# Two-layer gated cross-attention with routed experts: the last, partial chunk of keys packed by head, and its one odd key weighed by VectorE

## The reference, cut to what matters

```python
# M = 1601 context rows of 192, H = 16 heads of DH = 16
q = (x @ Wq + bq).reshape(B, N, 16, 16)
k = (y @ Wk + bk).reshape(B, M, 16, 16)
v = (y @ Wv + bv).reshape(B, M, 16, 16)
attn = softmax(einsum('bnhd,bmhd->bhnm', q, k) * 0.25, axis=-1)
out = einsum('bhnm,bmhd->bnhd', attn, v).reshape(B, N, 256)
```

## Time and profile before

| what | value |
|---|---|
| median of 3 runs | 1448.31 us |
| profiled execution, its own time | 1448.28 us |
| its span in the trace | 1446.5 us |
| PE, ACT, DVE busy (share of the span) | 92%, 68%, 41% |
| mean granted TensorE clock | 0.963 |
| attention of layer 0, first exp to last | 66.5 to 464.7 us |
| attention of layer 1, first exp to last | 765.7 to 1186.5 us |

### The profile page before, as it was taken

The page is one execution under the profiler, slowest core; times in us unless marked ns, Lnnn a source line. Parts: engine busy times, 40 slices in busy tenths (PEclk is TensorE's granted clock), DMA queues, the critical chain, the costliest instruction groups (busy, mean ns, idle before and its releaser), DMA issues. The chain is left out here.

```text
span 1446.5 us, 33184 instructions
## 1 busy us (share of the span) xinstructions
PE 1330.5 (92%) x13804; PEld 707.5 (49%) x13804; DVE 591.3 (41%) x1253; ACT 986.7 (68%) x1186; POOL 174.2 (12%) x188
## 2 busy tenths in 40 slices
PE   7799999999999999999968999999999986399994
PEld 4333333333433555999832333333334325399983
DVE  7412243152333344334361222652662665444435
ACT  4599999999998233223258996996996980155532
POOL 2000000000000331233300000000000000176540
PEclk9899999999999999999978999999999997599998
DMA  7671010010100912311349010110111215022214
GB/s 211 164 128 28 20 28 21 21 27 16 31 24 19 311 60 90 125 48 48 97 104 202 23 27 17 35 28 17 34 28 49 67 36 170 19 70 70 70 60 174
DMA packets 66273, 101.96 MB, mean 70 GB/s; under 512 B 10218, under 2 KB 48366, under 8 KB 65224
## 3 DMA queue, kind: packets, MB, share of 16 engines
q1 hardware_dynamic: 60168, 83.52, 20.9%
q0 software_dynamic: 5952, 16.26, 3.5%
HBM read 69.04 MB, written 26.21 MB: 66 GB/s over the span
## 5 line engine op out<-in xcount | busy, mean ns | idle before, releaser
L1327 ACT ACTIVATE arena<-ps 128x1024 f32<-128x1024 f32 x556 | 562.0, 1276 | 40.3 <-PE ps L1059 39.8
L1059 PE MATMUL ps<-arena 99*32 99x512 bf16 x6656 | 466.3, 384 | 14.9 <-PEq L869 11.0
L1059 PEld LDWEIGHTS ps<-arena 99*32 99x32 bf16 x6656 | 156.8, 95 | 398.0 <-issue 155.7
L1327 ACT ACTIVATE wqkv<-ps 128x1024 f32<-128x1024 f32 x276 | 302.3, 1278 | 16.8 <-PE ps L1059 16.7
L1075 PE MATMUL ps<-arena 128*32 128x512 f32 x2224 | 290.8, 594 | 1.1 <-ACT arena L1327 0.8
L1423 DVE COPY work<-ps 128x512 f32<-128x512 f32 x30 | 20.7, 691 | 322.7 <-PE ps L1075 322.6
L1909 PE MATMUL ps<-work,arena 128*128 128x128 f32 x1184 | 147.7, 281 | 2.7 <-DVE work L2001 1.5
L1909 PEld LDWEIGHTS ps<-work,arena 128*128 128x128 f32 x1184 | 146.5, 197 | 6.9 <-DVE work L2001 4.0
L1075 PE MATMUL ps<-wqkv,arena 128*32 128x512 f32 x1104 | 144.1, 593 | 0.1
L993 POOL DMA_INDIRECT work<-xn_img,fetch x62 | 60.2, 972 | 570.6 <-DVEq L1039 526.0
L1923 PE MATMUL ps<-arena,work 128*128 x496 | 117.3, 380 | 0.0
(11 more groups left out here) (219 smaller groups left out, 1186.0 us busy)
## 6 DMA issues: line engine op xcount, KB each, us to landing
arena<-in_ew SPq DMA_DIRECT2D x16, 512.0 KB, 5.8
arena<-q_img SPq DMA_DIRECT2D x32, 192.0 KB
arena<-y_tok SPq DMA_DIRECT2D x12, 512.0 KB, 6.4
arena<-k_img SPq DMA_DIRECT2D x8, 624.0 KB, 12.9
q_img<-work SPq DMA_DIRECT2D x18, 256.0 KB, 2.7
k_img<-work SPq DMA_DIRECT2D x21, 208.0 KB, 2.4
arena<-q_img SPq DMA_DIRECT2D x32, 128.0 KB
arena<-in_rg SPq DMA_DIRECT2D x8, 512.0 KB, 7.4
```

The costliest lines, as they stand in the source:

```text
L1059: last = nc.tensor.matmul(ps[i * VW:(i + 1) * VW, buf + j, :], k2[0:ROWS + SHIFT, h, at:at + VW], q2[0:ROWS + SHIFT, h, :], start=True, st ...
L1327: nc.scalar.activation(probs[(b * STEPS + u) % RING], ps[:, buf:buf + 2, :], ACT.Exp, scale=SCALE).then_inc(s_exp, 1)
```

## The change

The first 12 chunks of a group stay as they are. Chunk 12 is made anew:

- Its first unit holds the 64 whole keys of all four heads: bank `buf + j` has head `2j` in partitions 0 to 63 and head `2j + 1` in 64 to 127. It is again 8 matmuls and one exp of 128 x 1024.
- Its second unit is key 1600 alone: 4 matmuls, one per head, whose weights are that one column of `k2` read 32 times (`broadcast_to`), into one bank, and one exp of 128 x 512 into `last_exp`, which lies over `xn`.
- `weigh` of chunk 12 still has 4 matmuls; `v_aug` has values and ones for even heads in partitions 0 to 63, for odd heads in 64 to 127, and zeros in the others.
- `group` and `last_group` of DVE begin with `pv_sb = last_exp * last_v + bank` (a `scalar_tensor_tensor`), then the shuffle reads `pv_sb`; the plain copy goes. `last_v` holds the values of key 1600 per head and dimension, and a 1 in the sums' row.
- To make `last_v`: `project_v` of chunk 12 runs three pieces (two of 64 keys, one of a single key) instead of one, `copy_v` of chunk 12 three ACTIVATEs instead of one, SP stores the row to DRAM (`store_last_row`, behind a new wait on `s_va`) and loads it back by 4 DMAs of 16 partitions (`load_last_values`, behind the loads of group 1). DVE sets the rest of `last_v` in layer 0's preparation; `pad_v` has 6 memsets instead of 3.
- The ring `probs` advances by 25 slots a group, not 26, and ACT's wait on `s_pv` is computed from that.

```diff
@@ -56,6 +56,9 @@
 OUTPUT_AT = [(7, 9, 11, 13), (11, 12, 13, 14)]
+HALF = P // 2
+UNITS = 2 * NC
+READ = UNITS - 1
@@ -94,6 +97,7 @@
+        last_value = [nc.dram_tensor(f"last_value{l}", [D], F32).ap() for l in range(2)]
@@ -115,6 +119,7 @@
         top2 = sb("top2", [P, 2])
+        sum_row, last_v = sb("sum_row", [P, 1]), sb("last_v", [P, NG])
@@ -194,7 +199,9 @@
         hidT, at = view(work, at, [4, QB])
+        last_row = work[0:1, at:at + D]
         y_tmp, at = view(work, at, [2 * D])
+        last_exp = xn[:, (NB - 1) * TB:NT, :].rearrange("p t d -> p (t d)").rearrange("p (g q) -> p g q", q=QB)
@@ -331,6 +338,7 @@
         s_kones = keep("key_ones_set")
+        s_lrow, s_lv = keep("last_row_stored"), keep("last_values_in")
@@ -381,21 +389,48 @@
-            for ki in range(2):
-                last = nc.tensor.matmul(ps[:, bank, 0:D], ctxT[0:CH + ki, ki, c * P:(c + 1) * P],
-                                        wv[0:CH + ki, ki, :], start=(ki == 0), stop=(ki == 1))
+            if c < NC - 1:
+                pieces = [(ps[:, bank, 0:D], slice(c * P, (c + 1) * P))]
+            else:
+                keys = slice(c * P, c * P + HALF)
+                pieces = [(ps[0:HALF, bank, 0:D], keys), (ps[HALF:P, bank, 0:D], keys),
+                          (ps[0:1, bank, D:2 * D], slice(M - 1, M))]
+            for to, keys in pieces:
+                for ki in range(2):
+                    last = nc.tensor.matmul(to, ctxT[0:CH + ki, ki, keys], wv[0:CH + ki, ki, :],
+                                            start=(ki == 0), stop=(ki == 1), skip_group_check=True)
...
-            return nc.scalar.activation(v_aug[:, c, :, 0:DH], ps[:, bank, 0:D].rearrange("p (h d) -> p h d", d=DH),
-                                        ACT.Copy)
+            if c < NC - 1:
+                return nc.scalar.activation(v_aug[:, c, :, 0:DH],
+                                            ps[:, bank, 0:D].rearrange("p (h d) -> p h d", d=DH), ACT.Copy)
+            for i in range(2):
+                rows = slice(i * HALF, (i + 1) * HALF)
+                nc.scalar.activation(v_aug[rows, c, i::2, 0:DH],
+                                     ps[rows, bank, 0:D].rearrange("p (h d) -> p h d", d=DH)[:, i::2, :], ACT.Copy)
+            return nc.scalar.activation(last_row.rearrange("a (j d g) -> a g j d", j=HG, g=NG),
+                                        ps[0:1, bank, D:2 * D].rearrange("a (g j d) -> a g j d", j=HG, g=NG), ACT.Copy)
+        def store_last_row(eng, l):
+            eng.dma_start(last_value[l].rearrange("(a n) -> a n", a=1), last_row).then_inc(s_lrow, 16)
+        def load_last_values(eng, l):
+            eng.wait_ge(s_lrow, 16 * (l + 1))
+            by_row = last_value[l].rearrange("(j d g) -> j d g", g=NG, j=HG)
+            for j in range(HG):
+                eng.dma_start(last_v[j * VW:j * VW + DH, :], by_row[j]).then_inc(s_lv, 16)
...
             chain(nc.gpsimd.memset(v_aug[:, 0:NC - 1, :, DH:DH + 1], 1.0))
-            chain(nc.gpsimd.memset(v_aug[0:M - (NC - 1) * P, NC - 1, :, DH:DH + 1], 1.0))
+            for i in range(2):
+                own, other = slice(i * HALF, (i + 1) * HALF), slice((1 - i) * HALF, (2 - i) * HALF)
+                chain(nc.gpsimd.memset(v_aug[own, NC - 1, i::2, DH:DH + 1], 1.0))
+                chain(nc.gpsimd.memset(v_aug[other, NC - 1, i::2, 0:DH], 0.0))
@@ -589,6 +624,9 @@
                 sp.wait_ge(s_w, 16 * (5 if mlp else 3))
+                if l == 0:
+                    sp.wait_ge(s_va, NC)
+                    store_last_row(sp, 0)
@@ -802,6 +840,9 @@
                     nc.vector.tensor_copy(head_rows[:, :], head_sum[:, :]).then_inc(s_head, 1)
+                    chain(nc.vector.tensor_reduce(sum_row[:, :], ident[:, :].rearrange("p (j r) -> p j r", r=VW)
+                                                  [:, :, DH:DH + 1].rearrange("p j a -> p a j"), AX.X, ALU.add))
+                    nc.vector.tensor_copy(last_v[:, :], sum_row[:, :].broadcast_to([P, NG]))
@@ -1018,6 +1059,16 @@
+            def in_ring(b, u):
+                g, k = divmod(u, UNITS)
+                return (b * NG + g) * READ + k
+            def weighed_of(n):
+                g, k = divmod(n, READ)
+                return g * NC + k // 2
@@ -1052,13 +1103,21 @@
                                 pe.wait_ge(s_exp, b * STEPS + last_read + 1)
-                            for j in range(2):
-                                h = HG * g + 2 * half + j
-                                for i in range(4):
-                                    at = c * P + i * VW
-                                    last = nc.tensor.matmul(ps[i * VW:(i + 1) * VW, buf + j, :],
-                                                            k2[0:ROWS + SHIFT, h, at:at + VW], q2[0:ROWS + SHIFT, h, :],
-                                                            start=True, stop=True, skip_group_check=True)
+                            if c == NC - 1 and half:
+                                tiles = [(0, j, HG * g + j, k2[0:ROWS + SHIFT, HG * g + j, M - 1:M]
+                                          .broadcast_to([ROWS + SHIFT, VW])) for j in range(HG)]
+                            elif c == NC - 1:
+                                heads = [(j, i, HG * g + 2 * j + i // 2, c * P + i % 2 * VW)
+                                         for j in range(2) for i in range(4)]
+                                tiles = [(j, i, h, k2[0:ROWS + SHIFT, h, at:at + VW]) for j, i, h, at in heads]
+                            else:
+                                heads = [(j, i, HG * g + 2 * half + j, c * P + i * VW)
+                                         for j in range(2) for i in range(4)]
+                                tiles = [(j, i, h, k2[0:ROWS + SHIFT, h, at:at + VW]) for j, i, h, at in heads]
+                            for j, i, h, keys in tiles:
+                                last = nc.tensor.matmul(ps[i * VW:(i + 1) * VW, buf + j, :], keys,
+                                                        q2[0:ROWS + SHIFT, h, :],
+                                                        start=True, stop=True, skip_group_check=True)
@@ -1072,8 +1131,12 @@
                         for j in range(HG):
+                            if c < NC - 1:
+                                exps = probs[in_ring(b, 2 * w + j // 2) % RING][:, j % 2, :]
+                            else:
+                                exps = probs[in_ring(b, 2 * w) % RING][:, j // 2, :]
                             last = nc.tensor.matmul(ps[j * VW:(j + 1) * VW, 6 + g % 2, :], v_aug[:, c, HG * g + j, :],
-                                                    probs[(b * STEPS + 2 * w + j // 2) % RING][:, j % 2, :],
+                                                    exps,
@@ -1315,16 +1378,25 @@
                 def _(act):
+                    freed = 0
...
                         for u in range(STEPS):
-                            w, half = divmod(u, 2)
+                            g, k = divmod(u, UNITS)
...
                             act.wait_ge(s_qk, b * STEPS + u + 1)
-                            if half == 0 and b * NG * NC + w >= RING // 2:
-                                act.wait_ge(s_pv, b * NG * NC + w - RING // 2 + 1)
-                            nc.scalar.activation(probs[(b * STEPS + u) % RING], ps[:, buf:buf + 2, :],
+                            if k == READ:
+                                if b * NG + g >= 2:
+                                    act.wait_ge(s_u, b * NG + g - 1)
+                                nc.scalar.activation(last_exp[:, g % 2, :], ps[:, buf, :], ACT.Exp, scale=SCALE
+                                                     ).then_inc(s_exp, 1)
+                                continue
+                            n = in_ring(b, u)
+                            if n >= RING and weighed_of(n - RING) + 1 > freed:
+                                freed = weighed_of(n - RING) + 1
+                                act.wait_ge(s_pv, freed)
+                            nc.scalar.activation(probs[n % RING], ps[:, buf:buf + 2, :],
@@ -1420,12 +1492,15 @@
                         dve.wait_ge(s_pv, b * NG * NC + NC * (g + 1))
-                        nc.vector.tensor_copy(pv_sb, ps[:, 6 + g % 2, :]).then_inc(s_copy, 1)
-                        nc.vector.stream_shuffle(out=sums, in_=ps[:, 6 + g % 2, :], mask=[DH] * VW).then_inc(s_u, 1)
+                        if b == 0 and g == 0:
+                            dve.wait_ge(s_lv, 16 * HG * (l + 1))
+                        nc.vector.scalar_tensor_tensor(out=pv_sb, in0=last_exp[:, g % 2, :], scalar=last_v[:, g:g + 1],
+                                                       in1=ps[:, 6 + g % 2, :], op0=ALU.mult, op1=ALU.add
+                                                       ).then_inc(s_u, 1)
                         dve.wait_ge(s_u, n)
+                        nc.vector.stream_shuffle(out=sums, in_=pv_sb, mask=[DH] * VW).then_inc(s_copy, 1)
+                        dve.wait_ge(s_copy, n)
```

(14 more changed lines are left out.)

## The result

The changed kernel takes **1441.20 us** (median of 6 runs, 1437.81 to 1443.46) against 1448.14 for the kernel before beside it (6 runs, 1445.31 to 1451.61): ratio 0.9952, interval 0.9932 to 0.9973. That is 6.9 us saved, 3.9 to 9.8 by the interval. The forecast was 1438.3, the range 1436.7 to 1443.8. The profiled execution took 1443.46 us (span 1441.7), so it is one of the longer ones.

The account below looks back on a forecast made before the run. ACT was taken to bound 26 of 32 group ends, PE the other 6. Terms 12.1 - 0.3 - 0.8 - 0.9 - 0.1 = 10.0 us saved from the median 1448.31 gave 1438.3 us, range 1436.7 to 1443.8.

Parts of the forecast that it names:

- Part 1, the price of the short exp: Score loops on ACT: the exp of 128x512 costs 0.49 us instead of 0.916, saving 0.426 a group.
- A: Rival: weight loads not hidden in key 1600's unit, 0.60 us of PE instead of 0.215; 1440.6 us in all; chance 0.12.
- C: Rival: key 1600's four matmuls run one after another, 1.24 us; 1462 us in all; chance 0.05.
- B: Rival: PE bounds every group's end, so 6.9 us saved in place of 12.1; 1443.5 us in all; chance 0.10.
- D: Rival: the short exp's cost barely falls with its length; 1449.1 us in all, no change; chance 0.02.
- Part 1, the sum: Score loops: 26 ACT-bound groups save 0.426 us each, 6 PE-bound ones 0.215; 12.1 taken, 11.8 to 12.4.
- the scores three units on: Score loops: the scores waiting for the short exp lie three units on and come sooner or equal; no cost.
- The half term for group 2 of layer 0: Group end behind the router's pieces: at worst only PE's 0.215 saved, 0.6 us less in all; half taken.
- Part 2, late `oT`: Block's first output piece: DVE's 0.14 us longer group end may delay it in 6 blocks; 0.3 taken, 0 to 0.8.
- Part 2, the end of layer 1: Behind layer 1's last group: the product-sum goes in front of the shuffle with nothing to hide it, 0.8 us lost.
- Part 3, the values: Preparation before layer 0: chunk 12's `project_v` in three pieces costs 0.9 us, pieces of 64 keys side by side.
- Part 3, between the layers: Preparation of layer 1: the same extra work on values is hidden behind waits of ACT and PE; costs nothing.

Follow-up runs that it names:

- e6: Changed kernel with key 1600's unit back at 8 matmuls, 4 of them into a bank nobody reads: 1440.63 us, ratio 0.9943.
- e8: Changed kernel with a second, unused exp of 128x512 ahead of the short one, undoing ACT's saving: 1451.77 us, ratio 1.0026.
- e2: Changed kernel with the count of score banks carried over the block boundaries: 1439.07 us, ratio 0.9939.
- e3: Kernel before the change with only the count of score banks carried over the block boundaries: 1446.35 us, ratio 0.9989.
- e10: Kernel before the change with 80 one-column matmuls (160 PE instructions) ahead of the second jump: 1450.06 us, ratio 1.0012.
- e12: Kernel before the change with 8 one-column fp32 matmuls (32 PE instructions) ahead of the first jump: 1444.69 us, ratio 0.9986.
- e5: Changed kernel with 48 one-column matmuls (96 PE instructions) ahead of the second jump: 1438.84 us, ratio 0.9930.
- e11: Changed kernel with 128 one-column matmuls (256 PE instructions) ahead of the second jump: 1440.82 us, ratio 0.9952.
- e1: Changed kernel run again, unedited: 1440.07 us, ratio 0.9951.
- e4: Changed kernel with the four loads of the last key's values behind all group loads in SP's queue: 1440.65 us, ratio 0.9953.

## Why the prediction was right, and where it wasn't

The sign, the size within the range, and the mechanism were right. By its own steps:

- **Part 1, the price of the short exp** (0.49): 0.48. A group of 26 units bound by ACT takes 23.41 where it took 23.83, as forecast (23.4). The four matmuls run in one round, so A and C fall. The stretch from group 0's last exp to group 1's, where PE bounds, takes 24.27 in layer 0 where it took 24.48, which is the 0.215. e6 speaks against B, e8 against D.
- **Part 1, the sum** (12.1): blocks 1 and after save 1.26 in layer 0 and 1.37 in layer 1; with 4 * 0.426 for each block 0 (counted, since their stalls hide it) that is 3 * 1.26 + 3 * 1.37 + 3.4 = 11.3. The step that failed is the sentence "the scores three units on": at a block's first unit it is two, right behind the short exp. That took 0.8 (e2, e3). The half term for group 2 of layer 0, 0.1 a block, is there: the group behind it takes 23.51 where others take 23.41, and e6 shows that PE bounds it.
- **Part 2, late `oT`** (0.3, up to 0.8): it came in one block alone, and not by the step that the prediction gave. PE's timeline at the first output piece, layer 0 blocks 1 and 2:

```profile
173.66 1.03 PE L1138 MATMUL ps<-arena 128*32 128x512 f32 x8
175.14 1.07 PE L1171 MATMUL ps<-w,work 128*32 128x256 f32 x16 [0.45 <-issue]
...
273.47 1.03 PE L1138 MATMUL ps<-arena 128*32 128x512 f32 x8
274.33 1.03 PE L1171 MATMUL ps<-w,work 128*32 128x256 f32 x16
```

  The piece starts 1.48 behind the weighing and not 0.86, and block 1 is 0.64 longer than block 2. In the variants that is 0.3 to 0.8, in e6 nothing, and in e10, whose loops are the old ones, 0.3. PE waits for the last of the four DMAs: its semaphore is complete at 175.05, and PE's record of the wait ends at 175.08. From issue to landing this DMA takes 3.4 us in block 1 and 1.9 in block 2. The queues from 171.65 to 173 and from 271.75 to 274:

```profile
q8 instruction: 1, 0.02, 5.8%
...
work<-work SPq DMA_DIRECT2D x1, 32.0 KB, 3.4
```

```profile
q14 instruction: 1, 0.01, 1.4%
...
work<-work SPq DMA_DIRECT2D x1, 32.0 KB, 1.9
```

  In block 1 a 16 KB packet of the queue `instruction` moves from 172.63 to 173.88, and the last data packet of the DMA starts at 173.86. In block 2 there is one of 8 KB, and the DMA isn't late. All 18 stalls of 0.2 us or more in the first group of a block 1 to 3, in the 14 profiles, have such a packet between the first issue and the last landing, those of the old code too; in e6's block 1 it is over at 171.20, before the last issue ends. Where none falls in, DVE's 0.14 costs nothing. So the wait was the one that the prediction named, the cause was not, and that its 0.3 is near the cost is luck.
- **Part 2, the end of layer 1** (0.8): 1183.72 - 1182.18 = 1.54 against 0.75 in the earlier trace rows, and PE's wait grew from 6.87 to 7.65, 0.8. The end of layer 0 cost nothing, as said.
- **Part 3, the values** (0.9): from the first of these matmuls to L796 60.04 - 52.78 = 7.26, against 58.12 - 51.88 = 6.24 in the earlier trace rows, so 1.0. That the two pieces of 64 keys run side by side, as it assumed, fits. The remaining 0.9 of the 1.9 in the table was there before the values began (52.78 against 51.88); the old code starts them between 51.80 and 53.15 in four profiles, so that part is scatter.
- **Part 3, between the layers** (nothing): the values' extra work is hidden there, as said, but the stretch is longer. DVE's first update of `x` waits for the loads of `y_tok`, in the kernel before, the changed one and e6:

```profile
717.99 2.57 DVE L2063 SCALAR_TENSOR_TENSOR x<-arena,tgate,x 128x1024 f32<-128x1024 f32 x2 [8.06 <-DMA arena<-y_tok]
```

```profile
714.12 2.56 DVE L2146 SCALAR_TENSOR_TENSOR x<-arena,tgate,x 128x1024 f32<-128x1024 f32 x2 [9.55 <-DMA arena<-y_tok]
```

```profile
712.26 2.58 DVE L2146 SCALAR_TENSOR_TENSOR x<-arena,tgate,x 128x1024 f32<-128x1024 f32 x2 [8.00 <-DMA arena<-y_tok]
```

  In nine of the ten profiles with the change a 16 KB packet of the queue `instruction` moves while these loads and the next are under way, and the first `scales` are done 18.8 to 19.3 us after the first value matmul. In the four of the old code, and in e6, which has the change but 128 instructions more ahead, there is none, and it is 17.1 to 17.4. So this cost goes with the length of the code and not with the values; that the packet causes it is inferred.
- **Not in the prediction: the jump.** PE's wait of 6.67 behind the preparation stood in the earlier trace rows and was taken as fixed. It isn't: 3.1 us of it come and go, in e12 with the length of the code ahead of it. At the second switch the changed kernel has the long jump in every profile that leaves its length of code alone (3.4 to 3.8 us against 0.35), and e5, e10 and e11 show why. At the first it won 3.1 in most, but not in e1 and e4. In the profiled execution the two nearly cancel, so the forecast's total came out better than its account deserved.

Like for like, both jumps short in their profiles: e5 is at 0.9930 of the kernel before and e12, the old code, at 0.9986. The difference of 0.0056 is 8.1 us for the mechanism with all its costs, where the prediction said 10.0. The two intervals together leave 5 to 11 us, so the medians can't tell the terms of the 1.9 apart. By the traces 0.8 is the slip and 0.1 the values, and the first `scales` between the layers come 1.7 later in e5 than in e12 (19.1 against 17.4 from the first value matmul).

The Trainium skill's rule ("TensorE: Matmul & The Clock Gate", Part 3, The mechanism), that a weight load overlaps running matmuls only if its row group differs, would have put four loads of 0.095 in front of the new round. The three rounds in 0.65 contradict it here as the 0.86 of the full units did.

## What to carry to other kernels

When an item of a double- or triple-buffered loop gets shorter, look at the places where the rotation breaks (a count that isn't a multiple of the buffers): the lead is smallest there, and a shorter neighbour makes it cost more. Carry the count through.

When a change alters how many instructions an engine has ahead of a jump, its price belongs to the error bar: here 3.1 us a jump, against 6.9 gained. A few idle instructions ahead of it tell in one run whether the time is the mechanism's or the placement's. Count them in the trace: an fp32 matmul has twice the records of a bf16 one.

When a wait for a DMA varies from profile to profile, look at what the other queues move at that moment, the queue `instruction` too.

## What was not expected of the hardware

A jump of PE over a conditional block took 0.34 to 0.48 us or 3.3 to 3.9, with nothing between, while DVE's and SP's records of the same jump took 0.05 to 0.07. At the second jump the price followed the number of instructions ahead, with the same result 256 apart: relative to the kernel before, 0 or 32 more: short; 96 fewer or 160 more: long. In each long jump a 16 KB packet of the queue `instruction` starts 1.0 to 1.5 us after the jump does, and the jump ends 1.3 to 1.4 after the packet; in the short ones there is none. The changed kernel has 112 of these packets to 28083 records of PE, its sequencer's included, which is 251 a packet, near the 256 of the period. That a long jump waits for code to be fetched is inferred from these times and from the pads; no run changes the fetch alone. At the first jump two profiles out of ten of the changed loops had the long price in spite of the short place, with the packet in them, so timing has a part there that wasn't found.

The same packets meet the kernel's own DMAs. The last DMA of `oT` took 3.4 us to land with one beside it and 1.9 without, and where such a packet falls moves with the number of PE's instructions: in layer 0's block 1 it starts 1.8 us behind the first of the four issues in the kernel before, and 0.9 behind it in e12, with 32 instructions more. A change of the code can so move a stall from one block to another without having anything to do with it.
